# Kernel with adaptive layer norm, spectral binding attention and top-2 experts: rebuilt opening and another order of the last block

## The reference, cut to what matters

```python
mod = (_silu(c) @ wmod).reshape(4, 6, 1, -1)
sa, ca, ga, sb, cb, gb = (mod[:, i] for i in range(6))
ga = (2 * (ga >= 0) - 1) * jnp.maximum(jnp.abs(ga), 0.25)      # gb likewise
h = _layernorm(x) * (1 + ca) + sa                              # x: 4 x 1024 x 256
query, keys, values = (unit_projection(h @ W.T + b) for ...)   # each frequency divided by |f| + 1e-8
s = jnp.cumsum(bind(keys, values), axis=1)                     # product of spectra, summed over the sequence
x = x + ga * unbind(s, query)                                  # product with the conjugate, inverse transform
h = _layernorm(x) * (1 + cb) + sb
x = x + gb * ffn(h)                                            # 8 experts, top 2 per token, swiglu, 256-512-256
```

## Time and profile before

| what | value |
|---|---|
| three runs before | 587.25, 587.58, 587.61 us; median 587.58 us |
| the profiled execution | 584.68 us, span 582.5 us, mean granted clock 0.954 |
| PE busy | 544.5 us, 93% |
| DVE busy | 473.1 us, 81% |
| ACT busy | 302.2 us, 52% |
| POOL busy | 282.8 us, 49% |
| DMA | 79.37 MB, mean 136 GB/s |

### The profile page before, as it was taken

How to read it: one execution, slowest core, us unless ns; L and a number is a source line. 1 busy time by engine, 2 the same in 40 slices (tenths; PEclk the granted TensorE clock), 3 DMA queues, 4 the chain that set the end, 5 groups by cost and what they waited for, 6 DMA issues and landing times.

```text
span 582.5 us, 13330 instructions
## 1 busy us (share of the span) xinstructions
PE 544.5 (93%) x4008; PEld 404.8 (69%) x4009; DVE 473.1 (81%) x1062; ACT 302.2 (52%) x514; POOL 282.8 (49%) x197
## 2 busy tenths in 40 slices
PE   9999999999999985779899999999999999999992
PEld 5544555655656552537588888888888888888881
DVE  1267889999999989999688888888888888888882
ACT  4777688889797863654433333333333333333330
POOL 0004033343423342000638878877878877777634
PEclk9988999999899987858899999999999999999997
DMA  8314544644735437833677897786886686786533
GB/s 313 126 45 155 153 136 109 203 132 136 208 103 176 115 120 219 309 64 70 162 121 107 136 152 118 136 132 116 145 157 109 134 139 121 136 155 112 88 45 36
DMA packets 82109, 79.37 MB, mean 136 GB/s; under 512 B 45140, under 2 KB 71892, under 8 KB 81816
## 3 DMA queue, kind: packets, MB, share of 16 engines
q0 software_dynamic: 16912, 31.74, 31.3%
q1 hardware_dynamic: 63864, 46.28, 29.9%
q10 hardware_dynamic: 1296, 0.87, 0.5%
HBM read 44.06 MB, written 22.23 MB: 114 GB/s over the span
## 4 chain that ended last, share of the span: by engine, by line
PE 72%; DVE 13%; ACT 4%; issue 4%; DMA 4%; POOL 2%; POOLq 0%; DVEq 0%; ACTq 0%
PE ps L807 30%; PE ps L826 14%; PE ps L551 13%; PE ps L610 3%; DMA out_rows<-w_stage,region 3%; PE ps L652 2%; PE ps L564 2%; PE ps L648 2%; PE ps L474 1%; DVE region L1293 1%; POOL out_rows L1749 1%; ACT region L976 1%; PE ps L482 1%; ACT region L923 1%; DVE region L1415 1%
## 5 line engine op out<-in xcount | busy, mean ns | idle before, releaser
L807 PE MATMUL ps<-region,w_sb 128*128 128x256 f16 (+1 forms) x1920 | 194.3, 261 | 0.9 <-DMA region<-region 0.4
L807 PEld LDWEIGHTS ps<-region,w_sb 128*128 x1920 | 170.4, 98 | 20.1 <-issue 2.1
L1749 POOL DMA_INDIRECT out_rows<-w_stage,region x71 | 126.4, 1780 | 60.4 <-DMA out_rows<-w_stage,region 22.8
L1739 POOL DMA_INDIRECT region<-h_scratch,region x71 | 91.8, 1292 | 67.7 <-DVE region L1576 45.0
L1178 ACT ACTIVATE region<-region 128x1024 f16<-128x1024 f32 (+1 forms) x40 | 38.5, 961 | 130.4 <-DVE region L1630 130.4
L826 PE MATMUL ps<-region 128*128 x852 | 99.6, 273 | 1.9 <-DVE region L1636 1.7
L1622 DVE TENSOR_SCALAR region<-ps,region 128x256 f32<-128x256 f32 (+1 forms) x160 | 64.4, 448 | 43.0 <-PE ps L807 41.2
L826 PEld LDWEIGHTS ps<-region 128*128 128x128 f16 x852 | 82.6, 98 | 13.1 <-issue 3.5
L1166 ACT ACTIVATE region<-ps,region 128x256 f32<-128x256 f32 (+1 forms) x160 | 63.0, 445 | 53.0 <-PE ps L807 49.5
L551 PE MATMUL ps<-region 128*128 128x512 f32 x192 | 84.2, 595 | 3.2 <-ACT region L923 3.2
L1723 POOL TENSOR_TENSOR region<-region 128x512 f32<-128x512 f32 x30 | 37.3, 1270 | 94.9 <-DVE region L1320 94.9
(11 more groups left out here) (238 smaller groups left out, 702.3 us busy)
## 6 DMA issues: line engine op xcount, KB each, us to landing
w_stage<-in_w SPq DMA_DIRECT2D x20, 512.0 KB, 3.7
region<-in_x SPq DMA_DIRECT2D x8, 512.0 KB, 7.3
out_rows<-region SPq DMA_DIRECT2D x8, 512.0 KB, 3.0
h_scratch<-gb_bc SPq DMA_DIRECT2D x4, 1024.0 KB, 6.8
h_scratch<-region SPq DMA_DIRECT2D x8, 512.0 KB, 3.2
region<-region POOLq DMA_DIRECT2D x7, 512.0 KB, 4.5
region<-in_ramp SPq DMA_DIRECT2D x1, 2064.0 KB, 11.1
region<-in_w SPq DMA_DIRECT2D x4, 512.0 KB, 6.6
```

The costliest lines, as they stand in the source:

```text
L807: mm = pe.matmul(ps[:, GV + 2 * half + a, (f % 2) * MT:(f % 2) * MT + wide], w, xg_t[:, s, xa * KD + k, 0:wide], start=(n == 0), stop=(n = ...
L1739: G.indirect_dma_start(out=xg_rows[:, t % XG, u, :], out_offset=None, in_=h_scratch, in_offset=bass.IndirectOffsetOnAxis(ap=idx, axis=0)). ...
L1749: G.indirect_dma_start(out=out, out_offset=bass.IndirectOffsetOnAxis(ap=scatter_idx[:, at:at + 1], axis=0), in_=y_sb[:, t % 2, u, :], in_o ...
```

## The change

**Weight chunks 0 to 2** leave ACT and PE. DVE makes both parts of each (`weight_chunk`, two instructions), one ahead of each of three `first_magnitude` additions of block 0, which now follow each square one by one. Loads 2 to 4 are issued by SP ahead of the table of the modulation. ACT takes block 0's roots in parts, between the squares, and DVE adds the epsilon.

**The modulation** is formed as 128 x 32 columns in 16 small products behind `project(1)`; POOL applies sign, floor and scale in seven small instructions; PE transposes the result between the second and the third result of `transform(1)` and waits there for POOL; ACT moves it out. The table in memory has another order of its dimensions.

**Round 0** has another order: `nyquist_cols(1)` first, the two pieces of chunk 3 around `nyquist_row(0)`, `project(2)` ahead of the inverse, eight products that only keep PE busy, `inverse(0)`, and then `transform(2)`. On DVE `unbind(0)` moves into `bind(1)`, between two of its products, and `magnitudes(1)` is done in two parts, the first inside `bind(0)`.

**The last block.** The x of block 7 is added by two products of 512 columns ahead of the inverse, `inverse(7)` stands ahead of the last weight piece, DVE's `top2(4)` goes behind `unbind(7)`, and ACT's order is rewritten. The float16 rows of block 7 get a home of their own, so they wait for neither the write nor the transposes of block 6. POOL fills the masks of the routing, behind `uk_ready` of block 7.

```diff
@@ psum_plan
         if t == -1:
-            items += [("ny", 0, 0), ("lo", 0, 0)]
+            items.append(("ny", 0, 0))
+            continue
         elif t == 0:
-            items += [("pre", 0, 0), ("ny", 1, 0), ("row", 0, 0), *(("lo", 1, i) for i in range(4))]
+            items += [("ny", 1, 0), ("pre", 0, 0), ("lo", 1, 2), ("row", 0, 0), ("lo", 1, 3)]
             continue
@@ sync
-            for n in range(2):
+            for n in range(5):
                 load_weights(sp, n)
-            sp.wait_ge(mod_ready, 6)
-            sp.dma_start(mod_tab, mod_rows.bitcast(I32)).then_inc(mod_out, 16)
+            sp.wait_ge(mod_copied, 2)
+            sp.dma_start(mod_tab.rearrange("m b (k q) -> (m b k) q", k=KD), mod_rows.bitcast(I32)).then_inc(mod_out, 16)
...
-            for n in range(2, 6):
-                load_weights(sp, n)
+            load_weights(sp, 5)
@@ tensor
+            def modulation_columns():
+
+                pe.wait_ge(wmod_in, 16)
+                for m in range(4):
+                    for kd in range(KD):
+                        for ke in range(KD):
+                            at = (2 + m) * D + kd * P
+                            mm = pe.matmul(ps[:, OUT, (m * KD + kd) * BATCH:(m * KD + kd + 1) * BATCH],
+                                           wmod_sb[:, ke, at:at + P], c_silu[:, ke, :],
+                                           start=(ke == 0), stop=(ke == KD - 1))
+                mm.then_inc(mod_mm, 1)
+
             def modulation_rows():
...
+                pe.wait_ge(mod_ready, 7)
+                pe.transpose(ps[0:MODS, OUT + 1, 0:P], mod_flat_cols, ident_sb[:]).then_inc(mod_tp, 1)
@@ transform
                     mm.then_inc(z_mm, 1)
+                    if t == 1 and i == 1:
+                        modulation_rows()
@@ inverse
+                if t == LAST:
+                    for h in range(2):
+                        pe.matmul(ps[:, OUT + h, :], ident_sb[:],
+                                  x_sb[:, t % XS, 2 * h:2 * h + 2, :].rearrange("p j d -> p (j d)"),
+                                  start=True, stop=False)
                 for j in range(TPB):
                     cols = ps[:, OUT + j // 2, (j % 2) * D:(j % 2 + 1) * D]
-                    if t == LAST:
-                        pe.matmul(cols, ident_sb[:], x_sb[:, t % XS, j, :], start=True, stop=False)
@@ tensor, order
                     nyquist_cols(0)
-                    modulation_rows()
                     project(1)
-                    low_piece(0, 0)
+                    modulation_columns()
+                    continue
                 elif t == 0:
                     transform(1)
+                    nyquist_cols(1)
                     nyquist_sums(0)
-                    nyquist_cols(1)
+                    low_piece(1, 2)
                     nyquist_row(0)
-                    low_piece(1, 0)
-                    low_piece(1, 1)
+                    low_piece(1, 3)
+                    project(2)
+                    pe.wait_ge(mod_copied, 2)
+                    pe.wait_ge(w_lo[0], 2)
+                    keep_warm(8, ident_h[:], w1_sb[:, HI, 0:BLK], OUT + 1)
                     inverse(0)
-                    low_piece(1, 2)
-                    low_piece(1, 3)
                     continue
...
-                low_piece(t + 1, 3)
+                if t < LAST:
+                    low_piece(t + 1, 3)
                 if t >= 0:
                     inverse(t)
+                if t == LAST:
+                    low_piece(t + 1, 3)
@@ scalar
+                    if t == 0 and c >= 1:
+                        first_root(c - 1)
+                    if t == 1 and c == 0:
+                        modulation_rows()
+                        split_weights(EARLY)
...
+            def first_root(c):
+
+                act.wait_ge(mag_part, c + 1)
+                nc.scalar.activation(mag[:, 0, c, 0:BLK], mag[:, 0, c, 0:BLK], ACT.Sqrt).then_inc(root_part, 1)
+
+            def first_roots():
+
+                act.wait_ge(ny_out, 1)
+                nc.scalar.activation(mag[:, 0, :, BLK:NB], mag[:, 0, :, BLK:NB], ACT.Sqrt).then_inc(root_part, 1)
+                act.wait_ge(mag_ready, 1)
+                nc.scalar.activation(mag[:, 0, QRY, 0:BLK], mag[:, 0, QRY, 0:BLK], ACT.Sqrt).then_inc(root_ready, 1)
@@ scalar, order
                 if t == -1:
-                    split_weights(0)
-                    roots(0)
-                    split_weights(1)
-                    modulation_rows()
+                    first_roots()
                     spectra(1)
-                    low_piece(0, 0)
+                    modulation_columns()
+                    continue
                 if t == 0:
+                    roots(1)
                     project(2)
+                    low_piece(1, 2)
                     normal_rows(2)
-                    low_piece(1, 0)
-                    low_piece(1, 1)
+                    low_piece(1, 3)
                     nyquist_row(0)
-                    roots(1)
-                    residual(0)
-                    low_piece(1, 2)
-                    low_piece(1, 3)
                     spectra(2)
                     split_weights(4)
+                    residual(0)
                     split_weights(5)
                     continue
...
+                if t == LAST:
+                    low_piece(t + 1, 1)
+                    gate(t - 2)
+                    std2(t - 1)
+                    low_piece(t + 1, 2)
+                    nyquist_row(t)
+                    last_residual(0)
+                    last_residual(1)
+                    split_rows(t - 1)
+                    low_piece(t + 1, 3)
+                    last_std(0)
+                    split_weights(2 * t + 4)
+                    last_std(1)
+                    continue
...
-            last_std(0)
-            last_residual(1)
+            split_weights(19)
             gate_rows(LAST - 1)
-            last_std(1)
@@ vector
+            def weight_chunk(n):
+
+                dve.wait_ge(w_in[stage_of(n)], 16 * arrivals(n))
+                hi, lo = parts_of(n)
+                V.tensor_scalar(hi, staged(n), SW, None, ALU.mult).then_inc(chunk_hi, 1)
+                dve.wait_ge(chunk_hi, n + 1)
+                V.scalar_tensor_tensor(out=lo, in0=staged(n), scalar=SW, in1=hi, op0=ALU.mult,
+                                       op1=ALU.subtract).then_inc(w_lo[n % 2], 2)
@@ bind
+                if t == 0:
+                    dve.wait_ge(root_part, 3)
+                    V.tensor_scalar(mag[:, s, VAL, :], mag[:, s, VAL, :], EPS_UNIT, None, ALU.add).then_inc(eps_ready, 1)
...
                 if t == 0:
-                    modulation()
+                    dve.wait_ge(root_ready, 1)
+                if t == 1:
+                    ln1_rows(2)
                 dve.wait_ge(den_ready, t + 1)
...
+                if t == 1:
+                    unbind(0)
                 dve.wait_ge(all_ready, t + 1)
                 V.reciprocal(rec, rec).then_inc(rec_ready, 1)
...
+                if t == 0:
+                    magnitudes(1, slice(KEY, QRY))
@@ vector, order
-            for t in range(-1, NBLK):
...
+            ln1_rows(1)
+            for c in range(3):
+                weight_chunk(c)
+                first_magnitude(c)
+            bind(0)
+            magnitudes(1, slice(QRY, QRY + 1))
+            nyquist_apply(0)
+            ln1_moments(2)
+            for t in range(1, NBLK):
+                bind(t)
+                residual(t - 1)
+                if t + 2 < NBLK:
+                    ln1_moments(t + 2)
+                if 3 <= t < LAST:
+                    top2(t - 3)
+                nyquist_apply(t)
+                if t + 2 < NBLK:
+                    ln1_rows(t + 2)
+                unbind(t)
+                if t == LAST:
+                    top2(t - 3)
...
             top2(LAST - 2)
+            last_moments(0)
             low_rows(LAST - 1)
...
+            last_moments(1)
@@ gpsimd
+            def masks():
+
+                pool.wait_ge(uk_ready, NBLK)
+                for mask, n in ((keep, C1), (keep2, C2)):
+                    G.memset(mask[:, :, 1:n + 1], 1.0).then_inc(masks_set, 1)
+                    G.memset(mask[:, :, 0:1], 0.0).then_inc(masks_set, 1)
+                G.memset(picked[:, :, 0:1], 0.0).then_inc(masks_set, 1)
...
+            def modulation():
+
+                pool.wait_ge(mod_copied, 1)
+                g = mod_each[:, 0::3, :]
+                G.tensor_scalar(mod_sign, g, 0.0, 2.0, ALU.is_ge, ALU.mult).then_inc(mod_ready, 1)
...
+                pool.wait_ge(mod_ready, 6)
+                G.tensor_tensor(g, mod_sign, mod_size, ALU.mult).then_inc(mod_ready, 1)
```

169 lines of the change are left out of this document (81 added, 88 removed).

## The result

The change makes the kernel slower: 591.66 us (median of four runs, 590.70 to 591.83) against 587.41 us (median of four, 587.15 to 587.61). The ratio is 1.0069, 95% interval 1.0052 to 1.0087, so about 4.1 us are lost where 6.2 were forecast as gained. The profiled execution took 591.83 us, span 590.0, mean granted clock 0.934 (before: 584.68, 582.5, 0.954). Single executions of one kernel differ in the stretch from the first gather of the experts to the end (305.6 to 310.4 us in the profiles of this case), which no edit touches; so I follow starts of single instructions, and judge totals by the ratios. One of the ten later executions of the changed kernel (597.90 us) fell in a slower state and is left out of its median and ratio.

The account below looks back on a forecast made before the run. PE and DVE were taken as full in steady blocks, so opening gains carry through. 6.4 (opening) minus 0.2 (last block) gave 6.2 us, subtracted from the 587.58 median: 581.4 us; range 578.3 to 584.4.

Parts of the forecast that it names:

- the third transform: End of the opening on PE: would start at 60.0 instead of 66.47, 6.4 us earlier.
- second transform starts: Transform(1) on PE, behind the columns, project(1) and the modulation's products: at 33.1 instead of 40.62, 7.5 us earlier.
- The first reciprocal: DVE in the opening: starts at 32.9 against 39.35, 6.4 us earlier, with three weight chunks covered by DVE's idleness.
- Sixteen small products, 1.84 as the sixteen of their kind: The modulation's products on PE, behind project(1) in the opening: 1.84 us in all, ending at 33.1.
- POOL's seven instructions: Modulation arithmetic in the opening: 0.3 us each, 2.1 in all from 33.4, with no stall of PE in transform(1).
- the slower rival: POOL over 1.35 us per instruction: seven take 9.4, stall passes 6.2, kernel slower than before; chance 0.03.
- POOL late: Transform(1) waits for POOL: at 0.8 us each, stall 2.4, time 583.8; with six more us first, 586.3; chance 0.10.
- The end of the sums: Block 0's running sums on DVE: end at 46.2 against 51.46, 13.3 us after the reciprocal.
- Behind the sums: Block 2's rows after the last magnitude at 46.9: roots, epsilon, a 0.7 product and 0.35 scale, done at 50.2.
- The filler: Eight float16 products on PE ahead of inverse(0): 1.8 us at 2.4 GHz, 3.5 at 1.2; middle taken, 2.6.
- The blocks: Steady blocks after the opening: same work and order, 0 change, plus or minus 1.1 us for one clock dip.
- The last block: Block 7's end: 0.4 us lost to ACT's later queue, 0.2 regained by masks; bounds 1.9 gained to 1 lost.

Follow-up runs that it names:

- second profile: The changed kernel, unedited, run and profiled once more beside later experiments; median 592.14 us, ratio 1.0051 to the kernel before.
- the kernel with the late transpose: Changed kernel with PE's modulation transpose behind the last result of transform(1) instead of the second, ACT's move later too; 588.58 us, ratio 1.0003 to the kernel before.
- the opening alone: Changed kernel with the last block's edits undone; 592.08 us, ratio 1.0062 to the kernel before.
- the rows early and the modulation's arithmetic on DVE: Changed kernel with block 2's moments and ln1_rows ahead of magnitudes(1), ACT reordered, POOL's seven instructions on DVE; 584.75 us, ratio 0.9963 to the kernel before.
- the last block alone: Kernel before with only the last block's edits; 587.30 us, ratio 0.9968 to the kernel before.
- with the rows early: Changed kernel with block 2's moments and ln1_rows ahead of magnitudes(1) on DVE, ACT reordered to match; 587.69 us, ratio 0.9974 to the kernel before.

## Why the prediction was wrong

The range ended at 584.4 and the chance given to a slower kernel was 0.03. Its main number, the third transform at 60.0, came out at 68.83. Three terms failed: the columns were priced at half, the clock behind them at nothing, and `magnitudes(1)` inside `bind(0)` at its work alone, without the wait that it then brought on DVE. By the prediction's own steps along the chain of block 2's rows, each against the profile, with the second profile of the changed kernel last:

| step | predicted | measured | adds | second profile |
|---|---|---|---|---|
| second transform starts | 33.1 | 35.9 | 2.8 | 35.2 |
| its first two results | 3.5 | 6.5 | 3.0 | 5.5 |
| wait for POOL | 0 | 0.4 | 0.4 | 1.4 |
| the transpose and the last four results | 7.2 | 7.2 | 0 | 7.2 |
| from its end (43.8; 50.0) to block 2's scale on DVE (50.2; 57.9) | 6.4 | 7.9 | 1.5 | 7.8 |
| normalisation and `project(2)` | 3.2 | 3.9 | 0.7 | 3.9 |
| filler | 2.6 | 3.4 | 0.8 | 2.7 |
| inverse, to the third transform | 4.0 | 3.6 | -0.4 | 3.5 |
| third transform | 60.0 | 68.8 | 8.8 | 67.1 |

**The first reciprocal** (32.9): right, at 31.99; all that starts 0.7 earlier in this execution. DVE's idleness did hold the chunks.

**"Sixteen small products, 1.84 as the sixteen of their kind"**: this is where it failed first, by a misread row. The row counts records, and a float32 product leaves two. It held eight products; the sixteen products of the modulation leave 32 records (L529) and cost 3.8 us even at the upper clock, 2.0 more than predicted. The same is visible in the transform: 24 records for twelve products. With 1.9 us for the clock, and 1.1 less since PE reached the columns at 30.27 and not at 31.33, that makes the 2.8 of the first step.

**The clock in the opening** was given no term. Before, PE's narrow columns (to 30.2 us) were followed by the modulation's records of 512 columns, with two slices at 0.62 and 0.53 and 1.00 from 34 on. Now narrow columns, transposes and 32 narrow records stand in a row, and the clock stays at 0.50 for 8 us. Four kernels bear this out: with full products between the groups (one), or the columns inside the first transform (three), the next two results take 3.7 us, in place they take 5.4 to 6.5. This is 1.9 us in the first step and the 3.0 of the second.

**POOL's seven instructions** (0.3 each, 2.1 in all, no stall): wrong by a factor of three, and nearly free for a reason not foreseen. They took 6.4 us (36.39 to 42.80), between the 3.2 of room and the 9.4 of the slower rival. The stall showed with 0.4 us since PE was itself slowed by the clock, and with 1.4 (the same kernel, second profile) to 3.2 us where PE was faster. The rival "POOL late" priced them at 0.8 (and seven took 0.92 each); it was right on the size. The delay of some 6 us that the Trainium skill's GPSIMD Engine Reference, section Instruction dispatch, gives for the first call of a routine does not show: the first of the seven starts 0.1 us behind ACT's move (36.39 against 36.30) and takes 0.56.

**The end of the sums** (46.2: 12.1 from the reciprocal as before, and 1.2 for the part of `magnitudes(1)` inside): 51.97. From the reciprocal they took 20.0 us. Of the 6.7 that are too many, 6.04 are the wait for block 1's squares, which came late with the second transform, and 0.75 a wait for PE's columns. So the whole lead of the reciprocal was gone before POOL got any work, and `unbind(0)`, forecast to end at 53.4, ended at 60.6. No run put the sums ahead of `magnitudes(1)`. An estimate from this trace: the binding products end at 42.4 and the sums need 2.4, so they would end near 44.8. POOL's four products would then lie before block 2's rows, and the 1.85 and 1.02 us below would be 0.69 and 0.17, 2.0 us less on that chain.

**Behind the sums** (50.2 for block 2's scale): the chain was laid out rightly, but two of its links share time with POOL's four products. DVE's product of 516 columns took 1.85 us instead of 0.7, and its four-column scale 1.02 instead of 0.17; ACT's normalisation waited for the latter. That this chain decides was the step that I passed over. `unbind(0)` was forecast at 53.4 and `project(2)` also at 53.4, so the two looked level; in fact both slid with the transform of block 1, and the second came last, with PE idle 4.68 us in front. Moving two short steps of block 2 into DVE's 6 us wait gave 4.5 us back.

**The filler** (2.6, at a mixed clock): 3.4, all of it at the lower level, since PE had idled ahead of it. Without it the inverse runs at the lower level instead; it costs 0.9 to 1.8 us net where PE is late and nothing where the inverse waits for POOL.

**The blocks** (0, plus or minus 1.1 for a dip): the delay grew from 2.4 to 4.3 us over blocks 1 and 2, with weight pieces at the lower clock (the granted clock was 0.65 and 0.50 from 82 to 86, and 0.63 and 0.52 from 106 to 110; in the kernel before it was 1.00 in both stretches). That is 0.8 beyond the bound.

**The last block** (0.2 lost): about right in its steps; from the last reciprocal to the first gather 0.3 us were gained. Taking off the 4.66 us that block 7 came late, the x products start at 231.7 (forecast 232.0), the inverse ends at 238.4 (238.9), `gate_rows(6)` ends at 245.6 (245.9) and DVE's first low part starts at 246.1 (246.5). One price was missing: DVE's own two products took 2.14 us, beside POOL's (1.28 before), and the inverse waited for what follows them.

The range was also written a little wide of its own bounds: 3.4 and 9.2 taken from 587.58 give 578.4 to 584.2. That changes nothing here.

What stays open: what the sums ahead of `magnitudes(1)` would give; how much of the loss the clock alone makes, since no run could set it; where the median of the kernel with the late transpose gains; and whether the last block's own gain (0.5 to 3.2 us) is kept beside the new opening, since the ratios of the changed kernel (1.0051, 1.0069) and of the opening alone (1.0062) don't tell it.

The fastest version measured is the changed one with the rows early and the modulation's arithmetic on DVE; it beats both kernels, but not clearly the kernel before with the last block alone.

## What to carry to other kernels

Count products by what one leaves in the trace, not by the row's count: a float32 product is two records here. A lead on one engine is worth what the next engine's last input allows; write down, for each instruction that ends a wait, which of its inputs comes last **after** the change, and move the short steps of the next block (moments, root, scale) into the wait that the change opens. Before a wait is placed ahead of other work on an in-order engine, price what stands behind it as if its input were late. And price an instruction by a row in which the same neighbours run.

## What the runs showed of the hardware

POOL's seven instructions of 8 to 16 columns took 0.56 to 1.24 us each beside DVE's products and 0.22 once DVE was done. Their ends follow DVE's: POOL's ended at 38.91 and 40.06, DVE's products of 1032 columns at 38.80 and 39.95. The other way round, DVE's product of 516 columns took 0.69 alone and 1.85 beside POOL's. The Trainium skill's page SBUF — State Buffer, section Who interferes with whom, says that a VectorE instruction with two inputs in SBUF contends with a GpSimd instruction that reads SBUF, over a shared pair of ports that only one of them holds at a time. The traces agree, with POOL's ends 0.11 us behind DVE's.

Full products between the narrow ones kept the granted clock at 1.00, and behind 3.24 us of idleness it was 0.50 nonetheless, from 44 to 48. In the changed kernel the idle 4.68 us ahead of `project(2)` were likewise followed by a granted clock of 0.50 from 60 to 64. Idleness is not the only thing that it follows: with the rows early it was 0.77 and 0.50 from 52 to 56, behind narrow columns (49.69 to 51.6) and with PE busy throughout.
